# Attention weights in quarters, x later, identity products first, the first batch's queries packed later

## What is computed

```
x = x + tanh(g_xattn) * xattn(layernorm(x), ctx)     # ctx: 16 x 361 x 512
x = x + tanh(g_ffn) * (routed(layernorm(x)) + shared(layernorm(x)))

xattn: q = x Wq^T;  k, v = ctx Wk^T, ctx Wv^T (interleaved)     # 32 heads of 16
       q, k = rmsnorm over each head;  out = softmax(q k^T / 4) v
routed: 8 experts, top 1, SwiGLU 512 -> 1024 -> 512, times sigmoid(top logit)
```

## Time and profile before

| | |
|---|---|
| median of 3 runs | 971.75 us (970.72 to 972.25) |
| span of the profiled execution | 971.6 us |
| TensorE matmul busy | 945.1 us, 97% |
| TensorE weight load busy | 783.8 us, 81% |
| VectorE | 625.5 us, 64% |
| ScalarE | 548.7 us, 56% |
| GpSimd | 173.9 us, 18% |

### The profile page before, as it was taken

The page is one execution under the profiler, slowest core; times in us unless marked ns, Lnnn a source line. Parts: engine busy times, 40 slices in busy tenths (PEclk is TensorE's granted clock), DMA queues, the critical chain, the costliest instruction groups (busy, mean ns, idle before and its releaser), DMA issues. The chain is left out here.

```text
span 971.6 us, 24830 instructions
## 1 busy us (share of the span) xinstructions
PE 945.1 (97%) x10541; PEld 783.8 (81%) x10541; DVE 625.5 (64%) x1450; ACT 548.7 (56%) x839; POOL 173.9 (18%) x206
## 2 busy tenths in 40 slices
PE   5999999999999999999889999999999999999997
PEld 4777767777777777777777998999988988988886
DVE  6887655856558655676566444344577777777774
ACT  4677676677676677676632121221356666666653
POOL 1002121121113122113242300000111123112211
PEclk9999999999999999999999999999999999999999
DMA  8454634655445655356462311011387787788762
GB/s 315 103 117 91 110 85 91 142 95 107 88 104 133 146 89 117 76 101 139 100 139 97 90 31 36 23 44 56 125 253 216 236 239 231 215 235 240 225 208 63
DMA packets 175403, 129.98 MB, mean 134 GB/s; under 512 B 114610, under 2 KB 152498, under 8 KB 175288
## 3 DMA queue, kind: packets, MB, share of 16 engines
q1 hardware_dynamic: 165864, 108.60, 45.2%
q0 software_dynamic: 6544, 16.46, 5.5%
q10 hardware_dynamic: 2880, 3.29, 1.0%
HBM read 88.79 MB, written 13.56 MB: 105 GB/s over the span
## 5 line engine op out<-in xcount | busy, mean ns | idle before, releaser
L585 PE MATMUL bank<-arena_f32r 128*128 128x512 f32 (+1 forms) x1308 | 331.2, 403 | 13.0 <-DVE arena_f32r L948 11.4
L585 PEld LDWEIGHTS bank<-arena_f32r 128*128 128x128 f32 (+1 forms) x1308 | 231.9, 183 | 75.4 <-DVE arena_f32r L900 10.6
L779 ACT ACTIVATE probs<-score_banks 128x1600 f32<-128x1600 f32 x96 | 144.9, 1509 | 46.6 <-PE score_banks L604 46.1
L1691 ACT ACTIVATE hT_hi<-arena_f 128x224 fp32r<-128x224 f32 (+2 forms) x96 | 42.2, 441 | 117.4 <-DVE arena_f L1702 117.4
L1630 PE MATMUL bank<-xnT,arena_f32r 128*128 128x224 f32 (+1 forms) x720 | 103.5, 295 | 0.0
L1630 PEld LDWEIGHTS bank<-xnT,arena_f32r 128*128 128x128 f32 x720 | 97.8, 192 | 1.9 <-issue 0.8
L1702 DVE TENSOR_TENSOR arena_f<-bank,arena_f 128x224 f32<-128x224 f32 (+2 forms) x93 | 41.2, 443 | 65.8 <-PE bank L1630 65.3
L619 PEld LDWEIGHTS bank<-probs,values 128*17 128x17 f32 (+1 forms) x3072 | 63.6, 97 | 23.4 <-issue 21.5
L619 PE MATMUL bank<-probs,values 128*17 128x100 f32 (+1 forms) x3072 | 79.1, 251 | 0.8 <-ACT probs L779 0.8
L1056 POOL TENSOR_TENSOR heads_out<-heads_out,inv_sum 100x256 f32<-100x256 f32 x30 | 30.3, 1010 | 209.1 <-DVE inv_sum L1019 209.1
L1592 DVE TENSOR_TENSOR arena_f32r<-arena_f,arena_f32r 128x1024 fp32r<-128x1024 f32 x43 | 52.7, 1225 | 18.7 <-ACT arena_f32r L1585 18.7
(11 more groups left out here) (282 smaller groups left out, 1803.4 us busy)
## 6 DMA issues: line engine op xcount, KB each, us to landing
arena_f<-L_ffn_w_gate_up SPq DMA_DIRECT2D x48, 512.0 KB, 4.5
arena_f<-L_ffn_w_down SPq DMA_DIRECT2D x24, 512.0 KB, 4.0
arena_f<-ctx SPq DMA_DIRECT2D x15, 722.0 KB, 4.3
w_raw<-L_ffn_w_gate_up SPq DMA_DIRECT2D x16, 512.0 KB, 4.0
w_raw<-L_ffn_w_down SPq DMA_DIRECT2D x8, 512.0 KB, 5.4
x_all<-x SPq DMA_DIRECT2D x8, 400.0 KB
x_rows<-x_all SPq DMA_DIRECT2D x4, 800.0 KB
x_all<-x_rows POOLq DMA_DIRECT2D x4, 768.0 KB, 6.4
```

Of the source, the lines that this page charges most:

```text
L585: product = PE.matmul(bank[0:rows, :], src[:, j, 0:rows], weight, start=(m == 0), stop=(m == 11))
L779: A.activation(k.probs[n % 2][:], k.score_banks[:, :, 0:GH * k.N].rearrange("p j (r n) -> p j r n", r=GH), ACT.Exp, scale=float(HD) ** -0. ...
L1691: A.activation(k.hT[it % 2][0][:, j, 0:width], k.hidden[j][:, 0:width], ACT.Copy).then_inc(r.h_high, 1)
```

## The change

Weights come and are split in quarters of 128x512, twelve in all, with one semaphore for each of the eight quarters of the stage. `WEIGHT_SLOTS` has twelve entries: all of the values' and keys' quarters are split before the second context tile. SP loads the first quarter of Wv, the first context tile, the other seven quarters, the rest of the context, and only then the first two tiles of x; the statistics of the first x tile move from the first slot to j = 3 on VectorE. TensorE first multiplies the identity by itself 26 times into a bank that the scores use later. And in `FIRST_PLAN` the slots of the queries (the last of the four numbers) and of key tile 1 (the second) are later, the turn of key tile 1 now ahead of that of the queries.

```diff
-WEIGHT_SLOTS = (-7, 0, 1, 1, 12, 13)
+WEIGHT_SLOTS = (-7, -4, -3, -2, -1, -1, 0, 0, 12, 12, 13, 13)
+WARM_PRODUCTS = 26
...
-                  root_last=(3, 2), scale_slots=(22, 22, 31, 22), high_slots=(23, 23, 32, 23),
-                  low_slots=(23, 24, 33, 24), turn_slots=(23, 25, 33, 24))
+                  root_last=(3, 2), scale_slots=(22, 22, 31, 24), high_slots=(23, 24, 32, 26),
+                  low_slots=(23, 25, 33, 27), turn_slots=(23, 25, 33, 27))
...
+def pe_warm(k, PE, w):
+
+    w.wait_ge(k.ident32_made, 2)
+    for n in range(WARM_PRODUCTS):
+        PE.matmul(k.bank[7][:, 0:P], k.ident32[:], k.ident32[:], start=True, stop=True)
+
+
 def pe_attention(k):
     PE, w = k.PE, Waits(k.PE)
+    pe_warm(k, PE, w)
...
-    w.wait_ge(k.w_low, 2 * which + j // 2 + 1)
+    w.wait_ge(k.w_low, k.KD * which + j + 1)
...
-    kind, half = divmod(n, 2)
-    j = slice(2 * half, 2 * half + 2)
+    kind, j = divmod(n, k.KD)
...
-            elif s == (k.first_slot, prep_start(0) + 7)[c]:
+            elif s == prep_start(0) + (3, 7)[c]:
...
-def sp_load_weights(k, SP, w, kind, half):
-    w.wait_ge(k.w_low, 2 * (kind - 1))
-    j = slice(2 * half, 2 * half + 2)
-    SP.dma_start(k.w_stage[kind % 2][:, j, :], (k.w_v, k.w_k, k.w_q)[kind][:, j, :]).then_inc(k.weights_in[2 * (kind % 2) + half], 16)
+def sp_load_weights(k, SP, w, kind, j):
+    w.wait_ge(k.w_low, k.KD * (kind - 1))
+    SP.dma_start(k.w_stage[kind % 2][:, j, :],
+                 (k.w_v, k.w_k, k.w_q)[kind][:, j, :]).then_inc(k.weights_in[k.KD * (kind % 2) + j], 16)
...
-    sp_load_x(k, SP, 0)
     sp_load_weights(k, SP, w, 0, 0)
     sp_load_context(k, SP, w, 0, slice(0, 1))
-    sp_load_weights(k, SP, w, 0, 1)
-    for half in range(2):
-        sp_load_weights(k, SP, w, 1, half)
+    for j in range(1, k.KD):
+        sp_load_weights(k, SP, w, 0, j)
+    for j in range(k.KD):
+        sp_load_weights(k, SP, w, 1, j)
     sp_load_context(k, SP, w, 0, slice(1, None))
-    sp_load_x(k, SP, 1)
-    for half in range(2):
-        sp_load_weights(k, SP, w, 2, half)
+    for c in range(2):
+        sp_load_x(k, SP, c)
+    for j in range(k.KD):
+        sp_load_weights(k, SP, w, 2, j)
```

More of the change, by code:

```diff
@@ L296, in lay_out_semaphores @@
     k.ctx_in = [sem(f"ctx_in{i}") for i in ("_even", "_odd", "_rest")]
-    k.weights_in = [sem(f"weights_in{i}") for i in range(4)]
+    k.weights_in = [sem(f"weights_in{i}") for i in range(2 * k.KD)]
     k.gates_in, k.router_in, k.lists_cleared, k.table_out, k.x2_out = (
@@ L695, in act_weight_high @@
     src, high, _ = weight_views(k, n)
-    w.wait_ge(k.weights_in[n % 4], 16 * (n // 4 + 1))
+    w.wait_ge(k.weights_in[n % (2 * k.KD)], 16 * (n // (2 * k.KD) + 1))
     A.activation(high, src, ACT.Copy).then_inc(k.w_high, 1)
@@ L1218, in act_route_high @@
     if c < EARLY:
-        w.wait_ge(k.w_low, 6)
+        w.wait_ge(k.w_low, 3 * k.KD)
     t0 = k.N * (CT * c + j)
```

## The result

The changed kernel takes **974.49 us** (median of 6 runs, 974.16 to 976.63) against 971.66 us (6 runs, 970.72 to 972.25): ratio 1.0036, 95% interval 1.0027 to 1.0046, **2.8 us slower**. The profiled execution took 974.41 us, and its span is 972.4 us. So 2.0 us lie around the span; in the other runs of this case it is 1.9 to 2.3 us. By the same 2.0 us the profiled execution of the kernel before took about 973.6 us (an estimate), 1.9 us above its median: its span of 971.6 may not be set beside the median of the runs, as I did.

A forecast was written before the change was run, and what follows sets the result against it. TensorE, busy 97% of the span, was taken as the bound. -1.8 us at the start and +1.95 for late queries give +0.15; 971.75 + 0.15 + 0.9 for the clock = 972.8 us, range 970.3 to 974.5.

The forecast's parts named there:

- The loss at the queries: Before the first scores: the first batch's queries' turn, issued at 39.0 us, lands 1.95 us later; TensorE idles over 3 us.
- the 1.8 us won before that: Up to the queries' projection: 1.65 us won behind the turn of x, plus a 0.17 us wait that goes.
- The fall of the clock: Behind the wait for the queries' turn: a fall likelier than not, priced between 0 and 1.7 us, taken as 0.9.
- The base: Starting time of the sum: span 971.6 us set beside the runs' median 971.75 us, 0.15 us around it or noise.
- The identity block as free: Start of TensorE: identity products end at about 10.2 us, where real products begin today, so the block costs nothing.
- Quarters: Weight loading at the start: quarters land 0.7 us apart under the identity block and following products; data no longer bound them.
- The rival of slow quarters: Weight loading: SP's issue becomes the limit, x comes at 16 instead of 13, gain gone: 975 us, chance 0.04.
- The other rivals: Queries not late (0.10): 968.7 us; in-between landing (0.05): 970 to 971.5; identity block to 12.8 us (0.08): 973.5 to 974.4.
- What is won or lost by the first scores reaches the end: After the first scores: TensorE's slices are full, so any gain or loss by then carries to the end of the span.

The follow-up runs named there:

- e1: The changed kernel with the first batch's pack and turn slots of the kernel before: 972.63 us, ratio 1.0005.
- e2: The kernel before with only the first batch's slots of the changed kernel: 973.0 us, ratio 1.0024.
- e4: The changed kernel with x first and the old slots, leaving only identity products and quarters: 968.79 us, ratio 0.9972.
- e3: The changed kernel with the first tile of x loaded first again and its statistics in the first slot, new slots kept: 972.48 us, ratio 1.0012.
- e6: The changed kernel without the identity products: 972.06 us, ratio 1.0006.
- e8: The changed kernel with 8 more identity products in TensorE's wait for x: 973.71 us, ratio 1.0023.
- e10: e4 without the identity products, so quarters alone against the kernel before: 969.25 us, ratio 0.9978.
- e5: The kernel before with the 26 identity products added and nothing else: 970.14 us, ratio 0.9990.
- e9: e8 with ten more identity products before the first scores, so both waits are filled: 973.97 us, ratio 1.0030.
- e7: The changed kernel with key tile 1's turn issued behind the queries' turn: 973.71 us, ratio 1.0027.

## Why the prediction was wrong

The direction and most mechanisms were right, the size was not: 974.49 us is at the very edge of the range, and 1.05 us of loss were forecast where 2.8 were measured. The experiments split the 2.8: about 1.1 us is everything but the slots (e1 above the kernel before), and 1.7 to 1.9 us are the slots. The forecast had -1.8 for the first, and 1.95 and 0.9 for the second.

- **The loss at the queries** was forecast as 1.95 us and is 1.9 (e1, 1.9 between medians; 1.89 later in the trace). Issue at 39.0 (38.99 seen), the end of the old stall, and a wait of some 3 us before the scores (2.75) are as worked out. That the stall of 1.38 us would go and buy nothing is shown by e1 and e2.
- **The step that failed is the 1.8 us won before that.** When TensorE goes on behind the first turn, 0.9 us is won (18.74 against 19.65 us) where 1.65 was forecast, and at the second turn nothing (30.78 against 30.72). e2 has the start of the kernel before too, and its trace is at the second turn at 29.17 us: beside that one 1.6 us is lost. Two terms were off. x is ready at 18.1 us, not 17.4: the rest of the context is split from 13.09 us on, not 12.3, and everything behind it on VectorE moves along. TensorE's wait for it was 2.37 us, not 0.6. And behind that wait the clock fell. I had the wait at 0.6 us, since I let the identity products end at 10.2 us with 5.9 us of them slow. They ended at about 9.0, so TensorE came to x at 15.8 instead of 16.8 us and stood 2.4 us. The slow products cost 12.20 - 10.76 = 1.44 us (e4's 46 products beside these). A small slip of the working went the other way: behind the turn the next product starts 0.35 us later, not 0.6, so x at 17.4 gives 17.75 and not 18.0.
- **The fall of the clock** was forecast behind the queries' wait, with 0.9 us. In the changed kernel's trace it is behind the other one. e3 shows it where I had put it, at 2.45 us and more, above my upper bound of 1.7; e6 and e8 show it there too (14 products in 5.06 and 5.89 us), and the changed kernel's and e2's traces, with waits of 2.75 and 2.81 us, do not. The principle held, but where the clock falls changes from trace to trace, and I never asked it of the first wait. That the profiled run came out near the forecast for the queries' part, with no fall there, is luck.
- **The base was wrong.** I took the span, 971.6 us, for the time of the profiled execution. With 2.0 us around it that is 973.6, an execution slower than the median. Part of that is seen in the trace: the clock came up only 5.9 us after the first product, and the 28 products took 9.39 us, where e2, whose start is the same, took 8.03. The gain of the identity products, read from this trace, was more than the median has to give.
- **The identity block as free** was right for its place: e4's first product starts at 9.16 and e10's, without the block, at 9.26 us. It was not free for what came after: e6.
- **Quarters** were said to be hidden, data no longer the bound. e10 against the kernel before, 2.1 us, shows that they are the larger gain of the whole change (identity products alone: 1.0 us). With the identity products in both, e5 against e4, they are still worth 1.35 us. e10's trace has 0.8 us of it at the first product (9.26 against 10.06 us). I priced their pieces and left their gain at the start inside that of the block.
- The rival of slow quarters, for which a section of the Trainium skill spoke ("DMA: Bandwidth & Descriptors", section Bandwidth), is refuted for these transfers: e10, with quarters alone, is faster and not slower. The other rivals did not occur: the queries were late in every trace with the new slots, and the identity products ended at about 9.0 us.
- **"What is won or lost by the first scores reaches the end"** failed as well. From the first scores to the end of the span it is 930.0 us in the kernel before, 928.9 in the changed one, and 926.9 in e10. Three places make the difference:
  - A stall between 122 and 130 us. It is 0.40 to 0.52 us in the three traces e2, e6 and e10, and 0.90 to 1.93 in all others. ScalarE waits there for a turn of keys to land.
  - A wait of 1.98 us for ScalarE between 463 and 472 us, the one of the earlier trace rows. It stands in all twelve traces. Behind it the clock fell in the kernel before, the changed one, e4, e5 and e9, and stayed up in the other seven. From the end of this wait to the next one it is 12.84 us in e2, e6 and e10, and 14.3 in the kernel before and the changed one. So this fall costs 1.5 us, where the forecast read up to 1.7 from the earlier trace rows.
  - The stretch from there (480 to 485 us) to the end: 488.0 and 488.2 us in e2 and the kernel before, 487.0 to 487.4 in all others. That is the 1.1 us which the changed kernel has back against its first scores. One stall near 515 us is 1.8 and 1.6 us in these two, and at most 1.2 in the others.

```profile
471.06 0.54 PE L613 MATMUL score_banks<-qT,kT 32*128 32x100 f16 x32 [1.98 <-ACT probs L787]
...
485.36 0.88 PE L628 MATMUL bank<-probs,values 105*17 105x100 f32 x32 [0.80 <-ACT probs L787]
```

```profile
466.80 0.54 PE L612 MATMUL score_banks<-qT,kT 32*128 32x100 f16 x32 [1.98 <-ACT probs L786]
...
479.64 0.88 PE L627 MATMUL bank<-probs,values 105*17 105x100 f32 x32 [0.80 <-ACT probs L786]
```

The first pair is the changed kernel, the second e10. What stays open is whether the kernels without identity products (e2, e6, e10) keep these two gains for a reason or by chance: the kernel before has no identity products either, and has neither. One trace each does not tell.

## What to carry to other kernels

A stall that goes is a gain only if nothing stands behind it with no slack: look first for the wait that costs nothing today, here the queries' turn that landed as TensorE came. A warm-up block is worth what the engine does next: if its next input is late, it makes the wait longer, and a long wait can take the clock away again. A gain at the start is not yet one at the end: look at the later stalls of both traces too. And set a trace beside the median of the runs only when its own time is known.

## What the runs showed of the hardware

- A wait of 2.7 to 2.8 us for the queries' turn stands in five traces without work in it. Behind it the clock fell in three (2.74 us in e3, 2.73 in e8, 2.71 in e6) and stayed up in two (2.75 in the changed kernel, 2.81 in e2). In e3 the half clock lasted to the end of 14 products.
- A wait of 1.98 us near 470 us, in the same work, stands in twelve traces: the clock fell behind it in five and stayed up in seven. Waits of 1.79, 1.96 and 1.98 us near the start left it up (e6, e7); 2.37 us brought it down in the changed kernel and in e1.
- The kernels with a long wait for the queries spread widely from run to run: 971.5 to 978.1 us in e2, 970.0 to 974.6 in e6, 971.7 to 975.5 in e7, 971.3 to 974.8 in e8. In e2 and e7, which fall into two groups, the slower group has the lower mean clock, but for one run. e4, without such a wait, has 968.0 to 969.7.
- The full clock came at another moment in each run. Without identity products the first 28 products took 8.03 (e2), 8.48 (e6), 9.20 (e10) and 9.39 us (before), against 6.6 to 7.3 with them. The 52 instructions of the identity products took 7.5 to 8.5 us in these traces; all at full clock would be 5.7 us, an estimate from 0.11 us each.
